# A recommender tower on one core: a hold before the later chunks' gathers, another split schedule for the second chunk, and the turn of x1 behind the next select

## The reference, cut to what matters

```
e  = stack([tbl_f[ids[:, f]] for f in range(39)], axis=1)      # 512 x 39 x 16
x1 = einsum('bid,bjd,ijh->bhd', e, e,  W0)                     # 512 x 128 x 16
x2 = einsum('bid,bjd,ijh->bhd', e, x1, W1)
z  = sum(concat([x1, x2], axis=1), axis=-1)                    # 512 x 256
h  = relu(concat([z, dense_ctx]) @ W_top1 + b_top1)
y  = relu(h @ W_top2 + b_top2) @ W_top3
```

## Time and profile before

| what | value |
|---|---|
| median of 3 runs | 361.34 us (361.11 to 361.94) |
| the profiled execution | 362.48 us, its span 360.6 us |
| PE busy | 224.8 us, 62% of the span |
| DVE busy | 160.4 us, 44% |
| ACT busy | 158.7 us, 44% |
| POOL busy | 98.4 us, 27% (103 gathers) |
| mean granted clock of PE | 0.801 |

### The profile page before, as it was taken

How to read it: one execution, slowest core, us unless ns; L and a number is a source line. 1 busy time by engine, 2 the same in 40 slices (tenths; PEclk the granted TensorE clock), 3 DMA queues, 4 the chain that set the end, 5 groups by cost and what they waited for, 6 DMA issues and landing times.

```text
span 360.6 us, 4693 instructions
## 1 busy us (share of the span) xinstructions
PE 224.8 (62%) x1669; PEld 174.2 (48%) x1669; DVE 160.4 (44%) x333; ACT 158.7 (44%) x314; POOL 98.4 (27%) x107
## 2 busy tenths in 40 slices
PE   4311100000001010789997999999999999999997
PEld 4200000000000000656764678888788877888796
DVE  4350000000000100487896896767978758756311
ACT  4600000000000300378897875786877867766311
POOL 5777777777777750000000000000000000000000
PEclk9555555555555555599999999999999999999999
DMA  6900000000000000004720000000000000000000
GB/s 175 257 14 6 9 6 7 6 6 6 7 7 6 6 5 0 0 3 140 205 58 2 1 3 0 2 0 3 1 2 2 0 3 1 2 0 2 0 2 0
DMA packets 7835, 8.62 MB, mean 24 GB/s; under 512 B 2760, under 2 KB 5421, under 8 KB 7813
## 3 DMA queue, kind: packets, MB, share of 16 engines
q1 hardware_dynamic: 4516, 7.48, 7.4%
q0 software_dynamic: 3296, 0.85, 2.5%
HBM read 8.32 MB, written 0.00 MB: 23 GB/s over the span
## 4 chain that ended last, share of the span: by engine, by line
PE 55%; issue 34%; DVE 6%; another core or an unknown queue 2%; ACT 2%; DMA 1%; DVEq 0%; ACTq 0%
PE turn_bank L592 10%; PE x_bank L521 6%; PE pair_bank L493 6%; PE x_bank L524 5%; PE x_bank L523 5%; PE g_bank L555 3%; PE misc_bank L555 2%; DVE onehot L805 2%; PE x_bank L535 2%; PE turn_bank L630 2%; PE g_bank L720 2%; PE g_bank L572 2%; PE turn_bank L603 2%; PE turn_bank L720 1%
## 5 line engine op out<-in xcount | busy, mean ns | idle before, releaser
L463 POOL DMA_INDIRECT emb<-tbl,ids_sb x103 | 98.1, 953 | 33.6 <-issue 31.1
L1032 ACT ACTIVATE prod<-pair_bank 128x512 f32<-128x512 f32 (+1 forms) x108 | 63.5, 599 | 38.6 <-PE pair_bank L493 38.6
L882 DVE TENSOR_TENSOR prod_lo<-prod,prod_hi 128x512 fp32r<-128x512 f32 x92 | 61.8, 686 | 10.4 <-ACT prod_hi L1037 9.3
L521 PE MATMUL x_bank<-prod_hi,pair_w_hi 128*128 128x512 f32 (+1 forms) x108 | 61.5, 570 | 1.1 <-DVE prod_lo L882 0.7
L1143 ACT ACTIVATE looked<-pair_bank 128x192 f32<-128x192 f32 x2 | 0.6, 328 | 105.9 <-remote 105.9
L822 DVE COPY_PREDICATED looked<-odd,pair_bank 128x192 f32<-128x192 int32 x2 | 0.6, 369 | 97.7 <-issue 97.7
L493 PE MATMUL pair_bank<-x,sel 117*128 117x512 bf16 (+1 forms) x112 | 42.0, 384 | 1.2 <-ACT x L1010 0.7
L592 PE MATMUL turn_bank<-g_sb,w_sb 128*128 128x128 f32 x312 | 41.9, 277 | 0.0
L592 PEld LDWEIGHTS turn_bank<-g_sb,w_sb 128*128 128x128 f32 x312 | 40.0, 191 | 3.4 <-issue 1.0
L1037 ACT ACTIVATE prod_hi<-prod 128x512 fp32r<-128x512 f32 x64 | 40.4, 632 | 0.1
L720 PE MATMUL g_bank<-tab_parts,onehot 125*128 125x96 bf16 x36 | 6.9, 258 | 49.1 <-issue 49.1
(11 more groups left out here) (147 smaller groups left out, 364.3 us busy)
## 6 DMA issues: line engine op xcount, KB each, us to landing
emb<-tbl,ids_sb POOLq DMA_INDIRECT x103
tab<-small SPq DMA_DIRECT2D x2, 560.0 KB
wt<-w_top SPq DMA_DIRECT2D x2, 512.0 KB, 4.7
tab<-small SPq DMA_DIRECT2D x1, 504.0 KB
wa<-pair_w_a SPq DMA_DIRECT2D x1, 448.0 KB
wb<-pair_w_b SPq DMA_DIRECT2D x1, 448.0 KB
wtd<-w_dense SPq DMA_DIRECT2D x1, 256.0 KB
dense_sb<-dense_t SPq DMA_DIRECT2D x1, 256.0 KB
```

Of the source, the lines that this page charges most:

```text
L463: pool.indirect_dma_start(out=emb[:, at:at + D], out_offset=None, in_=tables[f], in_offset=bass.IndirectOffsetOnAxis(ap=ids_sb[:, c * M + ...
L521: mm = pe.matmul(x1_banks[k % 2][:, :], pair_w_hi[p, t, :], hi(n), start=(t == 0), stop=(t == FULL))
L882: dve.tensor_tensor(lo(n), prod[rows, n % RING, :], prod_hi[rows, n % RING2, :], ALU.subtract).then_inc(lo_done, 1)
L1032: act.activation(prod[0:ROWS[t], n % RING, :], pair_bank[n % 2][0:ROWS[t], :], ACT.Square).then_inc(sq_done, 1)
```

## The change

Three edits. The tiles of the second chunk's split change from (1, 2) and (6, 6) to (1, 4) and (5, 5). POOL waits, before the first gather of chunk 1, until the first chunk's turned x is kept (both adds to `x3_a`, the one to `x3_b`); the chunks after need no wait of their own. And `turn_x1(k - 1)` moves from the end of one step (u = 0) to the next step (u = 1), behind its `select_pair` and ahead of its `layer1`.

```diff
-SPLIT_AT = ((), ((1, 2), (6, 6)), ((0, 1), (3, 4)), ((0, 1), (3, 4)))
+SPLIT_AT = ((), ((1, 4), (5, 5)), ((0, 1), (3, 4)), ((0, 1), (3, 4)))
@@ gpsimd
             for c in range(NCH):
+                if c == 1:
+                    pool.wait_ge(x3_a, 2)
+                    pool.wait_ge(x3_b, 1)
                 for f in range(first_gathered(c), M):
@@ tensor, step(n)
                 if n < TILES:
                     select_pair(n)
+                if u == 1 and k >= 1:
+                    turn_x1(k - 1)
                 if m >= 0 and (not late or t >= LAG1):
                     layer1(m)
...
                 for part in look_at(n):
                     look_up_later(*part)
-                if u == 0 and k >= 1:
-                    turn_x1(k - 1)
```

## The result

The changed kernel takes 349.98 us (348.83 to 351.21) beside 361.23 for the kernel before (360.88 to 361.94): a ratio of 0.9685, interval 0.9664 to 0.9706. It is faster by 3.1%. The forecast was 255, with a range of 236 to 370: the direction is right and the range holds it, but the case that I chose is not the one that came.

What follows compares the result with a forecast made beforehand. Gathers were taken to slow PE in the head, and PE to bound the main part: 48.5 + 202.7 - 1.5 + 4.5 = 254.2 us of span, plus 0.7 for the median, gave 255; range 236 to 370.

Steps and rivals of the forecast that it cites:

- the crawl is PE's own: Head: something other than gathers slows PE, so the head stays 157.9 us and the hold only costs; 364 us, chance 0.27.
- head short, main part at its pace: Whole kernel: first select at 48.5 us, then the main part takes its 202.7 us beside gathers; 255 us, chance 0.50.
- the crawl moves along: Main part: gathers slow PE whatever it does, so the hold moves the crawl there; 364.5 us, chance 0.18.
- the sum: First select to end: 202.7 us of main part, -1.5 for x1, +4.5 for late gathers; 254.2 of span with the head.
- the first rival: Head: PE's crawl is its own, not caused by gathers, so the hold only costs; 364 us, chance 0.27.
- My lower bound, no lag: Head: PE recovers as soon as chunk 0's gathers end at 20.4 us, so the first select comes at 36.
- The price: Main part: later gathers 1.40 us apart make chunk 1 land 4.2 us late and chunk 3 cost 0.3 more, together +4.5.
- The factor of five: Main part: skill page's 620 against 3100 ns for descriptor generation beside DVE; would put chunk 3 some 100 us late; not used.
- -1.5 for x1: Main part: the moved turn of x1 lets a select hide waits for ACT's copy; -1.5 us, between -2.4 and 0.
- the term for the tiles: Chunk 1's split: starting at tile 5 wins up to 1.8 us if data were there; taken as 0, bound -1.8.

Runs made afterwards that it cites:

- e6: Changed kernel with the 89 gathers of chunks 1 to 3 replaced by six plain loads on SP's queue: 238.07 us beside 361.02, ratio 0.6594.
- e2: Changed kernel without the hold (the split's tiles and the turn of x1 alone), where the kernel before took 230.48: 229.37 us, ratio 0.9948.
- e1: Kernel before with the hold on POOL's later gathers alone, where the kernel before took 230.48: 235.44 us, ratio 1.0208.
- e14: Changed kernel without the hold (the split's tiles and the turn of x1 alone), where the kernel before took 361.65: 360.84 us, ratio 0.9974.
- e8: Changed kernel with the gathers of chunk c spread over the first 20 tiles of chunk c-1: 285.74 us beside 361.02, ratio 0.7879.

## Why the prediction was wrong

**Reading the head: right.** That PE's recorded starts are no guide to when its results arrive, that it crawled from 5 to 145 us, and that the gathers were behind it, all held: e6 takes the later gathers away and 112 us go. The case against, that the crawl is PE's own, had 0.27 and is out. The rule of the Trainium skill (SBUF — State Buffer, "Who interferes with whom") that I set beside it, that PE never waits on another user of SBUF, is not refuted by that: no run here shows that SBUF is where gathers and PE meet. It was no guide to the time.

**The step that failed** is the choice between two cases with the same head. I gave 0.50 to "head short, main part at its pace" and 0.18 to "the crawl moves along", and wrote against the second "only that no main part with gathers has been seen". The second came: from the first select to the end the sum had 202.7 - 1.5 + 4.5 = 205.7 us, and it took 314.5. The rows for it were in my own text: from 5 to 20 us PE slowed with DVE, ACT and DMA all busy. The row that I used against the first rival, a lag that outlives the gathers, told nothing on this choice. The rest of my weight on 0.50 had no row behind it, and should have gone to the case that a row bore out. Oddly, the forecast describes the other condition well: beside 230 the main part does run at its pace beside gathers (e2), but there is no long head to shorten either. That the kernel came out faster, as forecast, is luck: the forecast's reason, a main part at its pace, failed, and the 11 us are what the moved crawl is shorter than the old one. The range held 350 only because it was wide enough for both cases.

**The sizes in the case that came.** I had 364.5 for it (363.8 of span) and it took 350 (349.4 of span). The first select was put at 48.5 with the long lag of before (12.8 us after the last gather); it came at 34.9, 13.6 earlier, since after 14 gathers PE recovers within 2.3 us (20.9 to 23.1). My lower bound, no lag, was 36. At the far end, after 89 gathers in a row, the lag is back: 13.0 us, forecast as 12.8. So the lag came with the long rows only, and I had carried it over to a short one. The crawl was forecast to end at 172.6 and ended at 160.5, 12.1 earlier. The progress by then was put at 10 us and 1.5 more for the x1 edit; it was 202.7 - (349.4 - 160.5) = 13.8, which is 2.3 more. The two together are the 14.4 us.

**Gathers beside the main part.** Beside 230 this can be read cleanly: in e1 the gathers go from 26.5 to 147.1, 88 steps of 1.37 us, where I took 1.40 and bounded it by 1.25 and 1.70. The price was put at +4.5 us; the hold alone cost 5.0 and 4.0. The factor of five of the Trainium skill (SBUF — State Buffer, "A bandwidth-pool intuition that's wrong") is not what these runs show; the section has it for a `tensor_copy` on DVE, and my row, as the 92 operations of L882, is a sum or difference of two tensors, so it wasn't the section's case. And the mechanism is the one that the forecast and the first rival share: PE waits at chunk 1's turn for a split that waits for the last gather.

```profile
64.81 0.28 DVE L786 TENSOR_TENSOR rest<-emb 128x112 f32<-128x112 f32 x1 [0.96 <-DMA emb<-tbl,ids_sb]
...
65.74 0.52 PE L487 MATMUL x_bank<-idb,parts 128*117 128x128 bf16 x5 [2.16 <-ACT parts L1025]
```

These are rows of e1. Around this wait the granted clock is at its lower level for some us (0.66 on average from 65 to 70 us), a cost that I had not named and that no run sets apart:

```profile
65.00:70.00 5.00, 4.26 (x22) 2.91 (x23) 2.13 (x5) 1.86 (x4) 3.78 (x5) 0.66 0.08 10
70.00:75.00 5.00, 4.50 (x33) 2.78 (x32) 2.86 (x6) 3.72 (x9) 4.03 (x4) 1.00 0.08 7
```

**The split's tiles and x1.** I had -1.5 for x1 and up to -1.8 for the tiles where the data are there in time, so up to 3.3 together. Where they are (e14 and e2) the two won 0.8 and 1.1. The waits of line L535, 4.4 us in eight pieces before, are halved in e14:

```profile
  ACT x1h L1052: 2.2, 5
...
192.34 0.45 ACT L1021 ACTIVATE parts<-rest 128x112 bf16<-128x112 bf16 x1
...
193.00 0.46 PE L483 MATMUL x_bank<-idb,parts 128*117 128x128 bf16 x5 [1.64 <-ACT parts L1021]
```

and the wait at chunk 1's turn is 1.64 where it was 1.79. That doesn't mean that the tiles did nothing. Counted from the first select (157.66 here, 157.86 before), the last split on ACT (L1021) starts at 34.7 us in place of 35.9 (193.71 in the trace of before), PE comes to the turn at 33.7 in place of 34.7, and the turn starts at 35.3 in place of 36.5: both sides of the wait moved by about as much. This 1.1 us is all that the two edits win in this execution. The turns of chunks 2 and 3 are then 1.05 and 0.94 us earlier, so the moved turns of x1 win nothing more in the later blocks. Even if all of the 1.1 us were theirs, -1.5 was too much. How the 1.1 us divide between the tiles and the turns before them no run shows, as none has one edit without the other. And the term for the tiles was taken at 0 for a reason, late data, that holds only with the hold.

## What to carry to other kernels

When a suspect runs beside the victim only in one stage, moving the suspect elsewhere moves the damage unless a row shows the next stage immune; give that case the greater chance, and price both ends. Issue indirect gathers spread out over the work that hides them, tied to a count of finished tiles, rather than in one dense row; and time the kernel before again in every session, since the price of such a row was 130 us in one session and nothing in the next.

## What the runs showed of the hardware

- A long dense row of indirect DMAs from POOL (one each 1.26 us) can bring PE to one matmul each 2.80 us, while ACT and DVE, where they have work, keep their times (ACT's L1036 602 ns in the changed kernel, the same line 604 in e2). After a row of 89 or 103 PE needs 13 us to recover, after 14 it needs 2.3, after eight (e8) 1.3. In other sessions, one of them with the same chip number, the same program shows none of it (361.65 and 230.42 for the kernel before on chip 4). What differs between those sessions isn't known, and couldn't be set.
- Plain DMAs of the same size, issued by POOL at 549 ns each, cost PE nothing that shows (238.36, against 238.07 with six loads on SP's queue and 350.17 with the gathers), and neither scattered nor neighbouring rows matter in the indirect form (350.15). What the indirect form shares with PE wasn't found.
- PE's recorded starts can lead the release of its results by far: in the earlier trace rows the set recorded as started at 34.2 was released at 121.0. Whether the work or only its signal was that late no run tells, but the other engines go by the release, so the waits of the receivers are what to count with.
- The granted clock doesn't explain it: at 0.50 PE does lookups in 0.07 us each, and the crawl begins at 1.00. And a recorded clock can be wrong for a whole execution: e14's reads 1.00 throughout, though 14 matmuls take 3.00 us at one place and 1.70 at the next.
